# Projections of a transformer sandwich: layer norm on 33 distinct rows, normalisation moved to VectorE, unread products dropped

## The reference

```python
x = x + LN(dilated_attention(LN(x)))
x = x + LN(ternary_ffn(LN(x)))
x = x + LN(gated_attention(LN(x)))       # y below is its output, before LN
x = x + LN(gqa_and_experts(LN(x)))       # starts with rmsnorm, then q, k, v projections
```

## Time and profile before

| | us |
|---|---|
| median of 3 runs | 686.95 (686.89 to 688.94) |
| profiled execution, time | 687.56 |
| profiled execution, span | 685.8 |
| PE busy in the span | 548.0 (80%) |
| DVE busy | 506.5 (74%) |
| ACT busy | 360.7 (53%) |
| POOL busy | 268.0 (39%) |
| mean granted PE clock | 0.841 |

### The profile page before, as it was taken

The page is one execution under the profiler, slowest core; times in us unless marked ns, Lnnn a source line. Parts: engine busy times, 40 slices in busy tenths (PEclk is TensorE's granted clock), DMA queues, the critical chain, the costliest instruction groups (busy, mean ns, idle before and its releaser), DMA issues. The chain is left out here.

```text
span 685.8 us, 11832 instructions
## 1 busy us (share of the span) xinstructions
PE 548.0 (80%) x3800; PEld 307.6 (45%) x3800; DVE 506.5 (74%) x2314; ACT 360.7 (53%) x738; POOL 268.0 (39%) x499
## 2 busy tenths in 40 slices
PE   1866478838967699867999999999999898798870
PEld 1856367727656466411233333333333454455420
DVE  6599999371273678688989999999997155269784
ACT  5841134500120467601478878878878754456762
POOL 2001007720002267810254544555455454266774
PEclk9996565555897699955599999999999998899996
DMA  8000000000000038510011211111210000000001
GB/s 315 1 1 1 0 1 1 0 1 0 1 1 1 0 119 227 169 62 6 1 36 32 63 31 35 34 33 37 58 36 1 7 1 1 2 0 16 32 16 61
DMA packets 17580, 24.77 MB, mean 36 GB/s; under 512 B 3246, under 2 KB 14014, under 8 KB 17342
## 3 DMA queue, kind: packets, MB, share of 16 engines
q1 hardware_dynamic: 16942, 21.91, 10.4%
q10 hardware_dynamic: 576, 2.10, 0.8%
HBM read 13.65 MB, written 10.35 MB: 35 GB/s over the span
## 5 line engine op out<-in xcount | busy, mean ns | idle before, releaser
L905 DVE CUSTOM_DVE_ANT_0 w_qkvT<-d_pS,w_qkvT 128x512 bf16<-128x512 f32 x480 | 203.9, 486 | 16.7 <-PE d_pS L896 11.8
L1566 ACT ACTIVATE d_P<-d_pT 128x768 f32<-128x768 f32 (+1 forms) x192 | 165.9, 882 | 62.7 <-PE d_pT L1592 61.1
L1446 POOL TENSOR_SCALAR_AFFINE_SELECT d_P<-d_P 128x256 f32<-128x256 f32 x256 | 102.6, 415 | 134.0 <-ACT d_P L1566 133.9
L896 PE MATMUL d_pS<-Ks,Qs 48*128 48x512 bf16 x480 | 97.8, 324 | 12.8 <-DVE hadamard L905 8.9
L1592 PE MATMUL d_pO<-d_P,V 128*32 128x512 f32 (+3 forms) x1024 | 98.5, 460 | 1.4 <-POOL d_P L1446 0.9
L1592 PE MATMUL d_pT<-Qs,Ks 51*128 51x512 bf16 (+3 forms) x512 | 72.9, 312 | 2.0 <-ACT d_mT L1536 2.0
L896 PEld LDWEIGHTS d_pS<-Ks,Qs 48*128 48x128 bf16 x480 | 32.2, 96 | 56.1 <-DVE hadamard L905 51.9
L1592 PEld LDWEIGHTS d_pT<-Qs,Ks 51*128 51x128 bf16 x512 | 20.7, 95 | 74.1 <-ACT d_P L1566 42.3
L1930 PE MATMUL e_PE<-gate_expT,w_qkvT 128*128 128x512 f32 x96 | 44.8, 614 | 6.3 <-DVE e_T L1804 3.5
L1804 DVE SCALAR_TENSOR_TENSOR e_T<-e_PE,comb,e_T 128x128 f32<-128x128 f32 x128 | 35.2, 343 | 19.2 <-ACT e_T L1907 19.2
L1907 ACT ACTIVATE e_T<-e_PE,comb 128x128 f32<-128x128 f32 x128 | 36.1, 377 | 24.8 <-issue 14.5
(11 more groups left out here) (311 smaller groups left out, 1036.6 us busy)
## 6 DMA issues: line engine op xcount, KB each, us to landing
Qs<-q_stack SPq DMA_DIRECT2D x32, 192.0 KB, 3.1
q_stack<-Qp SPq DMA_DIRECT2D x8, 384.0 KB, 2.6
X<-in_x_dram ACTq DMA_DIRECT2D x4, 512.0 KB, 6.1
q_stack<-Qp SPq DMA_DIRECT2D x8, 256.0 KB, 2.5
out_dram<-e_moe SPq DMA_DIRECT2D x8, 256.0 KB, 2.0
w_qkvT<-in_w_qkvT_dram SPq DMA_DIRECT2D x1, 1536.0 KB
Ks<-k_stack SPq DMA_DIRECT2D x32, 48.0 KB, 3.2
q_stack<-Qp SPq DMA_DIRECT2D x8, 128.0 KB, 2.1
```

Source lines behind the costliest of these rows:

```text
L896: last = nc.tensor.matmul(dst[:, at:at + w], top.Qs[c][rows, h % 8, 128 * q:128 * q + 128], top.Ks[c][rows, h // 4 % 2, 0:w], start=True, ...
L905: last = nc.vector.tensor_tensor_reduce(out=junk[:, at:at + w], in0=src[:, at:at + w], in1=top.wide_mask[:, 512 - w:512], scale=1.0, scala ...
L1446: last = nc.gpsimd.affine_select(out=view, in_=view, compare_op=ALU.is_ge, fill=0.0, base=0, pattern=[[0, 2], [1, 128]], channel_multiplie ...
L1566: nc.scalar.activation(P[pair % 4][:, :, P_AT[unit]:P_AT[unit] + w], pT[(3 * pair + unit) % 2][:, :, 0:w], ACT.Exp, scale=float(HD4) ** -0 ...
```

## The change

Four things are changed in c.

- LN(y) moves ahead of the products. On the 33 distinct rows: Y_full = Y + yU; moments of Y_full and of yU; square root on ACT, reciprocal on DVE, both normalised in place, and Y rewritten as their difference. It is done once for each Q. PE's `attended` waits for it (`y_rows`). Per batch, the y statistics, the square root, the reciprocal, four scaled additions and two `shift` instructions go; one addition of 128x512 takes their place.
- `normed` (N4) goes from POOL to DVE, one turn later than the moments.
- The second part of k goes from ACT to POOL.
- `keep_busy` goes for batches 2 to 6; for batches 0 and 1 it is 8 products ahead of `by_channel` and none behind it.

Beside these, ACT starts the phase with a square root of its own, and DVE waits for `zeroed` in `values`, not at its start.

```diff
+                def row_moments(Q):
+                    nc.vector.tensor_tensor(Y_full[Q][:, :], top.Y[Q][:, :], top.yU[Q][:, :], ALU.add)\
+                        .then_inc(sm["y_full"], 1)
+                    dve.wait_ge(sm["y_full"], Q + 1)
+                    nc.vector.bn_stats(y_st[Q][:, 0, :], Y_full[Q][:, :])
+                    nc.vector.bn_stats(y_st[Q][:, 1, :], top.yU[Q][:, :]).then_inc(sm["y_stats"], 1)
+                    dve.wait_ge(sm["y_stats"], Q + 1)
+                    for j in two:
+                        last = nc.vector.bn_aggr(y_mv[Q][:, j, :], y_st[Q][:, j, :])
+                    last.then_inc(sm["y_mv"], 1)
+                def normalise_rows(Q):
+                    dve.wait_ge(sm["y_std"], Q + 1)
+                    nc.vector.reciprocal(y_rs[Q][:, :], y_std[Q][:, :]).then_inc(sm["y_rstd"], 1)
+                    dve.wait_ge(sm["y_rstd"], Q + 1)
+                    for j, row in enumerate((Y_full[Q], top.yU[Q])):
+                        last = nc.vector.tensor_scalar(row[:, :], row[:, :], y_mv[Q][:, j, 0:1], y_rs[Q][:, j:j + 1],
+                                                       ALU.subtract, ALU.mult)
+                    last.then_inc(sm["y_norm"], 1)
+                    dve.wait_ge(sm["y_norm"], Q + 1)
+                    nc.vector.tensor_tensor(top.Y[Q][:, :], Y_full[Q][:, :], top.yU[Q][:, :], ALU.subtract)\
+                        .then_inc(sm["y_rows"], 1)
+                def attended(n):
+                    dve.wait_ge(sm["y_psum"], n + 1)
+                    nc.vector.tensor_tensor(X[:, R * n:R * n + R, :], PY[n % 2][:, :, :], X[:, R * n:R * n + R, :],
+                                            ALU.add).then_inc(sm["x"], 1)
+                def normed(n):
+                    dve.wait_ge(sm["norm"], n + 1)
+                    for t in range(R):
+                        last = nc.vector.tensor_scalar(N4[:, R * n + t, :], X[:, R * n + t, :], x_mv[n][:, t, 0:1],
+                                                       rs[n][:, 0, t:t + 1], ALU.subtract, ALU.mult)
+                    last.then_inc(sm["n4"], 1)
...
                 for turn in TURNS:
...
+                    if turn - 1 in batches:
+                        normed(turn - 1)
+                    if turn in batches:
                         norm_scalars(turn)
...
                 def attended(n):
+                    pe.wait_ge(sm["y_rows"], n // 4 + 1)
                     wait(pe, sm["x"], n - 1)
...
                     if turn - 1 in batches[:LAST]:
-                        keep_busy(turn - 1, 4)
+                        if turn - 1 < 2:
+                            keep_busy(turn - 1, 8)
                         by_channel(turn - 1)
-                        keep_busy(turn - 1, 6)
                         project(turn - 1)
```

More of the change, by code:

```diff
@@ L926, in projection_phase @@
         ph = Phase(nc, ctx, "c_")
-        sm = ph.sems("rms_bias y_psum y_stats y_mv y_std y_rstd x y_shift shift x_stats x_mv std rstd norm a n4 aT_psum aT "
+        sm = ph.sems("rms_bias y_full y_stats y_mv y_std y_rstd y_norm y_rows y_psum x x_stats x_mv std rstd norm a n4 aT_psum aT "
                      "q_psum k_psum v_psum q1 k1 qr kr q2 k2 q3 k3 v_ready zeroed ones")
@@ L936, in projection_phase @@
         small = lambda name, *shape: [ph.sb(f"{name}{n}", [128, *shape]) for n in batches]
-        y_st, x_st, y_mv, x_mv = small("y_st", R, 6), small("x_st", R, 6), small("y_mv", R, 2), small("x_mv", R, 2)
-        y_std, y_rs, y_sh, nb = (small(name, R) for name in ("y_std", "y_rs", "y_sh", "nb"))
+        x_st, x_mv, nb = small("x_st", R, 6), small("x_mv", R, 2), small("nb", R)
+        Y_full = [ph.sb(f"Y_full{Q}", [128, D]) for Q in two]
+        y_st, y_mv = [ph.sb(f"y_st{Q}", [128, 2, 6]) for Q in two], [ph.sb(f"y_mv{Q}", [128, 2, 2]) for Q in two]
+        y_std, y_rs = [ph.sb(f"y_std{Q}", [128, 2]) for Q in two], [ph.sb(f"y_rs{Q}", [128, 2]) for Q in two]
         std, rs = small("std", 2, R), small("rs", 2, R)
@@ L974, in _, with other_parts @@
             def _(pool):
[L975 to L982, removed]
+                def other_parts(n):
+                    pool.wait_ge(sm["kr"], n + 1)
+                    nc.gpsimd.tensor_copy(Kp[n % 3][:, 1, :], Kr[n % 2][:, :]).then_inc(sm["k2"], 1)
                     pool.wait_ge(sm["k2"], n + 1)
@@ L997, in _ @@
                     if turn - 2 in batches:
-                        third_parts(turn - 2)
-                    if turn - 1 in batches:
-                        normed(turn - 1)
+                        other_parts(turn - 2)
             @block.vector
             def _(dve):
-                def stats(src, st, mv, n, s):
+                def row_moments(Q):
[8 more added lines that the diff above has]
+                    last.then_inc(sm["y_mv"], 1)
@@ L1005, in stats, with moments @@
+                def attended(n):
+                    dve.wait_ge(sm["y_psum"], n + 1)
+                    nc.vector.tensor_tensor(X[:, R * n:R * n + R, :], PY[n % 2][:, :, :], X[:, R * n:R * n + R, :],
+                                            ALU.add).then_inc(sm["x"], 1)
+                def moments(n):
+                    dve.wait_ge(sm["x"], n + 1)
                     for t in range(R):
-                        last = nc.vector.bn_stats(st[n][:, t, :], src(t))
-                    last.then_inc(sm[s + "stats"], 1)
@@ L1008, in stats @@
-                    dve.wait_ge(sm[s + "stats"], n + 1)
+                        last = nc.vector.bn_stats(x_st[n][:, t, :], X[:, R * n + t, :])
+                    last.then_inc(sm["x_stats"], 1)
+                    dve.wait_ge(sm["x_stats"], n + 1)
                     for t in range(R):
[L1010 to L1017, removed]
-                    for t in range(R):
[L1019 to L1032, removed]
+                        last = nc.vector.bn_aggr(x_mv[n][:, t, :], x_st[n][:, t, :])
@@ L1062, in maxima_ahead @@
                             .then_inc(top.scores["S_max"], 1)
-                dve.wait_ge(sm["zeroed"], 2)
+                for Q in two:
+                    row_moments(Q)
+                for Q in two:
+                    normalise_rows(Q)
                 nc.vector.memset(top.wide_mask[:, 0:384], 0.0)
@@ L1068, in _ @@
                 for turn in TURNS:
-                    if turn in batches:
-                        dve.wait_ge(sm["y_psum"], turn + 1)
-                        stats(lambda t: PY[turn % 2][:, t, :], y_st, y_mv, turn, "y_")
                     if turn - 2 in batches:
@@ L1075, in _ @@
                         attended(turn)
-                        dve.wait_ge(sm["x"], turn + 1)
-                        stats(lambda t: X[:, R * turn + t, :], x_st, x_mv, turn, "x_")
-                        shifts(turn)
+                        moments(turn)
+                    if turn - 1 in batches:
+                        normed(turn - 1)
+                    if turn in batches:
                         norm_scalars(turn)
@@ L1096, in normalise, with deviation_rows @@
                     last.then_inc(sm["a"], 1)
-                def deviation_y(n):
-                    act.wait_ge(sm["y_mv"], n + 1)
-                    nc.scalar.activation(y_std[n][:, :], y_mv[n][:, :, 1], ACT.Sqrt, bias=top.eps[:, :])\
+                def deviation_rows(Q):
+                    act.wait_ge(sm["y_mv"], Q + 1)
+                    nc.scalar.activation(y_std[Q][:, :], y_mv[Q][:, :, 1], ACT.Sqrt, bias=top.eps[:, :])\
                         .then_inc(sm["y_std"], 1)
@@ L1121, in first_parts, with second_part @@
                         nc.scalar.activation(part[n % 3][:, 0, :], ps, ACT.Copy).then_inc(sm[s1], 1)
[L1123 to L1126, removed]
+                def second_part(n):
+                    act.wait_ge(sm["qr"], n + 1)
+                    nc.scalar.activation(Qp[n % 3][:, 1, :], Qr[n % 2][:, :], ACT.Copy).then_inc(sm["q2"], 1)
+                nc.scalar.activation(nb[0][:, 0:1], top.eps[:, :], ACT.Sqrt)
+                for Q in two:
+                    deviation_rows(Q)
                 act.wait_ge(sm["rms_bias"], 1)
@@ L1131, in _ @@
                         normalise(turn - 1)
-                    if turn in batches:
-                        deviation_y(turn)
                     if turn - 2 in batches:
-                        second_parts(turn - 2)
+                        second_part(turn - 2)
                     if turn - 1 in batches:
```

2 lines of the change are left out of this document (added).

## The result

| | before | after |
|---|---|---|
| median of 4 runs each, taken together | 687.95 (686.89 to 689.06) | 701.04 (695.41 to 703.28) |
| profiled execution, span | 685.8 | 701.3 |
| mean granted PE clock | 0.841 | 0.809 |

The changed kernel is slower: ratio 1.0166, 95% interval 1.0121 to 1.0211. The forecast was 697.2 with a range of 683 to 706.

A forecast was written before the change was run, and what follows sets the result against it. PE was taken as the bound, its clock deciding. Start -1.0, turns -5.6 and tail +2.3 plus 26.5 c for the low-clock share, with c 0.55, gave +10.3: 697.2 against 686.95, range 683 to 706.

The forecast's parts named there:

- What bounds, and what sets the clock: Phase c: PE bounds the turn; unread 128-row products help bring up and hold the full clock; no size of its own.
- Start: Beginning of phase c to X of batch 2: -1.0 us, with bounds -7.7 and +1.5.
- The sign that was named for the start: Start of phase c: X of batch 0 ends 2 us earlier and PE's first PY waits for y_rows at about 222.
- Turns: Five turns from X of batch 2 to X of batch 7: -5.6 + 25 c us against 37.9.
- c: Share of the work in turns 3 to 7 at the low clock: 0.35 to 0.9 (chance 0.60), 0.55 chosen.
- The reading that a rise is caught by the k and q products: Turns without unread products: the clock rises only by the k and q products, in about half of the low turns.
- Tail: After X of batch 7, before the first maximum: +2.3 us, plus 1.5 c for batch 6's k product.
- two groups: Tail: two batches' scalings, before on POOL, now stand on DVE ahead of the first maximum, 2 x 1.13 us.
- Sum: Whole phase c: -1.0 - 5.6 + 2.3 + (25 + 1.5) c = -4.3 + 26.5 c, giving +10.3 us.
- An even clock: Rival, turns: clock falls in one turn of three, returns at once; c 0.1 to 0.35, 685 to 692, chance 0.18.
- a clock that holds: Rival, phase c: full clock holds, c from 0 to 0.1, -11.0 us, 676, up to 685; chance 0.20.
- The other engines as the bound: Rival, full-clock turns: DVE busy plus waits makes 6.3 us, 1 us in all; no separate chance given.

The follow-up runs named there:

- the padded kernel: Changed kernel with PY over 128 rows, zeros around each batch's own 32, and the Ks and V4 clearings behind these copies: 678.18, ratio 0.9848.
- the fifth run: Changed kernel with unread products back as before, plus GpSimd's clearing of Ks and V4 moved behind y_rows: 688.58, ratio 1.0004.
- the first experiment: Changed kernel with the unread products put back, 4 ahead of by_channel and 6 behind it in every turn: 687.89, ratio 1.003.
- the kernel of the last comparison: The padded kernel, batches 0 and 1 keeping 8 unread products, 16 added in turn 7 and around by_channel(7), normed all on DVE: 677.20, ratio 0.9838.
- the fourth run: Changed kernel with PY made over all 128 rows, other batches' rows added to y: 681.61, ratio 0.9919.

## Why the prediction was right, and where its terms were off

**What bounds, and what sets the clock: right, and shown.** PE bounds the turn (in the padded kernel together with the 0.69 us that it waits for ACT's copy), and the share of it at the low clock decides the sign. That the unread products held the clock was read from the stretches ahead of each fall and rise; it is now shown by putting them back (687.89), by taking only them away (700.54), by keeping them with 32 rows (724.94), and by giving `PY` 128 rows in their stead (681.61, 678.18).

**Start, predicted -1.0, measured -1.4 for X of batch 2: right by two errors that offset each other.** `y_rows` was to come at 222.0 and came at 224.3, 1.8 later in the phase. The step that failed is the price of the two scalings, 0.6 from the earlier trace rows: that row is of a scaling with POOL idle, and here POOL was clearing `V4`. The prediction knew of the clearing as the wait that the change moves away, and didn't ask what else it stands beside. On the other side `PY` of batches 0 to 2 took 9.2 us at the low clock (224.36 to 233.53), not 3 x 3.7: with nothing between them, the products of one batch overlap those of the next, which use other rows. The sign that was named for the start, X of batch 0 ending 2 us earlier, didn't come: it ended 9.6 us into the phase, 0.2 earlier than in before. In the fifth run, with the scalings at 0.35, it ended at 7.8, and there it is 2.0. Of the 5.98 us in the earlier trace rows about 1.0 lie ahead of the phase; no term of the sum rests on it.

**Turns, predicted -5.6 + 25 c: the form right, c too low.** The turn at the low clock was to take 10.9 and took 10.90. At the full clock the changed kernel had no whole turn to measure; the padded kernel's takes 5.90, against 6.15. The 6.15 summed durations of the earlier trace rows that include the overlap of one group with the next. From 49.0 us for the five turns, c is (49.0 - 32.3) / 25 = 0.67, where 0.55 was chosen: 3 us. This is the c of one execution, the slowest of four. If what the others took less were all in c, the median, 2.2 us below it, would have about 0.59 and the fastest 0.37: an estimate, which says that 0.55 was well inside what chance does here. The reading that a rise is caught by the k and q products held for the stretches at 249.76 and 280.48, but both lasted only 3.4 us. No cost was taken for DVE, ACT and POOL, and none shows: DVE 5.1 busy in 5.90, as worked out.

**Tail, predicted +2.3 + 1.5 c = 3.3 at the measured c, measured +4.5: the size near by luck, the composition wrong.** Three parts make the 4.5, each the difference of two distances. In before, the timeline of PE has these rows:

```profile
280.78 1.05 PE L1146 MATMUL c_PK<-c_aT,qkv4T 128*32 128x512 f32 x2 [0.50 <-ACT c_aT L1113]
...
282.72 0.97 PE L1146 MATMUL c_PT<-qkv4T,c_aT 128*128 128x32 f32 x8
```

From the end of X of batch 7 to the start of batch 6's k product it is 0.19 us there and 1.48 in after: +1.29. X stands earlier in its turn since DVE no longer takes the moments of y ahead of it, so PE is what DVE waits for. It is the same shift that made X of batch 2 early: a gain of the start that the tail gives back. From that product to the end of the v products, 2.91 becomes 5.46: +2.55 for the low clock, where the prediction had 1.5 c, for the k product alone. From there to the first maximum, 0.67 becomes 1.35: +0.68, for batch 7's scalings. Batch 6's are hidden behind ACT's cast, so "two groups" was wrong. That batch 7's group would be held by POOL's subtractions (2.5 us) shows in the kernels with a full clock there; in after it fell between two of them and took 1.1. At the full clock the tail is hardly shorter: 7.8 us in the first experiment and 7.4 in the kernel of the last comparison, 4.0 and 3.7 more than in before, where the prediction had 2.3. So what the tail costs is mostly `normed` on DVE and X's earlier place, and by these two less than 1 us of the 4.5 hangs on the clock.

**Sum.** -4.3 + 26.5 x 0.67 is +13.5, and the last maximum is 13.8 later in the phase. That is no check of its own, since c is worked back from the turns; it says that the errors of the other terms (start 0.4, tail 1.2, maxima 0.5) nearly cancel. What was off in the forecast of +10.3 is mainly c. The median rose by 13.1.

**The rivals.** An even clock and a clock that holds both fell with the trace of after; the faster one came true in form once `PY` had 128 rows, in another kernel: 678.18, against 676 foreseen for c = 0 (start -6.2 for -7.7, turns -6.8 for -5.6, tail and maxima +4.7 for +2.3). The other engines as the bound: not seen; at the full clock the padded kernel's turn takes 5.90, below the 6.3 of this rival, with DVE at 5.1 busy.

## What to carry to other kernels

Before an unread product is dropped, read what PE did ahead of each fall and each rise of the clock: a turn can be packed with products of few contraction rows and run at half speed. If the useful products are short of rows, lay them out over all 128, with zeros around them; they take the same time, and here they hold the clock without the ten products that nobody reads (5.90 against 7.27 us a turn). When work moves to VectorE, ask what GpSimd runs at that moment, clearings included, and check in the tail which of the moved groups DVE has no wait behind. When a total shows nothing, add up the stages: the first experiment's total equals that of before, and its tail is 4.0 us longer.

## What the runs showed of the hardware that was not expected

- Contraction rows count for the clock, and zeros count as well as data: PE busy in 13.62 of 13.62 us at 0.50 with 32-row unread products, 5.32 of 6.00 us at 1.00 with 128-row ones that are zero in 96 rows of one operand. Whether 64 rows would do was not tried.
- A float32 scaling of 128x128 on DVE took 2.35 us beside GpSimd's clearing of 128x3072, and 0.35 without it; four of them took 2.53 beside GpSimd's subtractions and 1.08 to 1.11 without. An addition with two tensors stood at 0.29 beside the clearing of `Ks`, and was not held. The Trainium skill, SBUF — State Buffer, SBUF: two separate sides, says that GpSimd and a DVE operation in a 2-port mode exclude one another for the whole instruction, and that an operation with two SBUF inputs is excluded only by a GpSimd operation that reads. The trace agrees where it can: the scaling ends 0.08 us behind the clearing of `V4` (223.92 and 223.84), and the addition wasn't held by a clearing, which reads nothing. That the scaling runs in such a mode, and what a GpSimd operation that reads does to an addition, no run here shows.
- Where float32 products on one group of 32 rows follow straight on those of another group, the last of one overlap the first of the other (in the timeline, rows of four where the others are of two): three groups of 8 took 9.17 us at the low clock, where one alone takes 3.71. With 128 rows, in the fourth run, every row of these products in the timeline is one of two. A row of four in the changed kernel:

```profile
227.09 0.80 PE L1163 MATMUL c_PY<-Y,selT 32*128 32x128 f32 x4
```
